# A tile's base product moved in among the expert tiles, and a split moved out of the layer that makes the data into the one that reads it

## The reference, cut to what matters

```python
def _L2_ffn_ref(x, base_w, base_b, A, B, router_w):
    base_out = jnp.einsum('bsi,oi->bso', x, base_w) + base_b
    res_hidden = jnp.einsum('bsi,ri->bsr', x, A)
    topw, topi = jax.lax.top_k(softmax(x @ router_w.T), 2)      # weights normalised, 16 experts
    delta = jnp.einsum('bse,bsr,eor->bso', combine, res_hidden, B)
    return base_out + delta * SCALING

def _L3_ffn_ref(hidden_states, ...):      # hidden_states = y3 = agg_w @ x + agg_b, channels mixed again
    h = jnp.maximum(hidden_states @ up_w, 0) ** 2
    shared_out = h @ down_w
    ...                                    # gates, latent experts
    return layernorm(shared_out + routed_out)

x = x + _L2_ffn_ref(...)
x = x + _L3_ffn_ref(_L3_cond_ref(x, ...), ...)
```

## Time and profile before

| | us |
|---|---|
| median of 3 runs | 1654.09 (1651.56 to 1657.61) |
| profiled execution | 1651.25 |
| its span, first to last instruction | 1649.5 |
| TensorE busy | 1576.2 (96%) |
| VectorE busy | 823.7 (50%) |
| ScalarE busy | 506.4 (31%) |
| GpSimd busy | 315.2 (19%) |
| mean granted clock of TensorE | 0.988 of 2.4 GHz |

### The profile page before, as it was taken

One profiled execution on the slowest core, in us unless ns is written; L12 is line 12 of the kernel. 1 busy time (PEld: TensorE's weight loads), 2 busy tenths in 40 slices (PEclk: granted clock), 3 DMA queues, 4 the chain that ended last, 5 costly groups with the idle time before them and its releaser, 6 DMA issues.

```text
span 1649.5 us, 20620 instructions
## 1 busy us (share of the span) xinstructions
PE 1576.2 (96%) x7752; PEld 1284.4 (78%) x7752; DVE 823.7 (50%) x1336; ACT 506.4 (31%) x761; POOL 315.2 (19%) x262
## 2 busy tenths in 40 slices
PE   7899879999998889999999999999999999999996
PEld 5688558889976558877888888887788888888875
DVE  4567578895374537772333333332723333333336
ACT  3344325333265521223222222212232222222122
POOL 1000022234155530122211111112112101111110
PEclk9999999999999999999999999999999999999999
DMA  9765635556774757894531111114925311111115
GB/s 308 224 197 166 139 97 182 167 186 212 243 241 126 288 194 291 301 321 155 111 92 51 51 51 51 51 52 140 319 77 100 83 49 51 51 51 51 52 41 177
DMA packets 117241, 238.57 MB, mean 145 GB/s; under 512 B 22503, under 2 KB 61551, under 8 KB 115778
## 3 DMA queue, kind: packets, MB, share of 16 engines
q1 hardware_dynamic: 80890, 154.75, 28.2%
q0 software_dynamic: 23008, 68.24, 13.8%
q10 hardware_dynamic: 13264, 14.52, 3.2%
HBM read 164.51 MB, written 89.19 MB: 154 GB/s over the span
## 4 chain that ended last, share of the span: by engine, by line
PE 77%; DVE 4%; POOL 2%; issue 2%; DMA 1%; ACT 1%; SPq 0%; ACTq 0%; DVEq 0%; POOLq 0%
PE pu L1956 27%; PE pd L1956 26%; PE l_po L1956 7%; PE pf L1956 6%; POOL scratch_pairs L1464 2%; PE l_ea L1313 2%; PE pw L648 2%; PE pw L647 2%; PE l_ea L1889 1%; PE l_po L1889 1%; PE pg L1085 1%; PE l_ea L1904 1%; PE l_tr L1904 1%; DMA scratch_g<-latent_out 1%; DMA scratch_expert_out<-expert_out,pair_ids 0%
## 5 line engine op out<-in xcount | busy, mean ns | idle before, releaser
L1956 PE MATMUL pd<-down_hi,hid_hi 128*128 128x512 f32 x640 | 249.1, 389 | 2.9 <-issue 2.9
L1956 PE MATMUL pu<-y_hi,up_hi 128*128 128x512 f32 x640 | 250.5, 391 | 0.6 <-issue 0.6
L1956 PE MATMUL pu<-y_lo,up_hi 128*128 128x512 f32 x640 | 250.3, 391 | 0.0
L1956 PE MATMUL pu<-y_hi,up_lo 128*128 128x512 f32 x640 | 250.3, 391 | 0.0
L1956 PE MATMUL pd<-down_hi,hid_lo 128*128 128x512 f32 x640 | 249.0, 389 | 0.0
L1956 PE MATMUL pd<-down_lo,hid_hi 128*128 128x512 f32 x640 | 249.0, 389 | 0.0
L2257 DVE TENSOR_TENSOR hid_lo<-hidden,hid_hi 128x512 fp32r<-128x512 f32 x64 | 44.3, 692 | 391.5 <-ACT hid_hi L2165 391.5
L2087 POOL TENSOR_TENSOR down_lo<-raw,down_hi 128x1024 fp32r<-128x1024 f32 x40 | 100.3, 2508 | 681.2 <-ACT down_hi L2102 681.2
L2159 ACT ACTIVATE hidden<-pu 128x512 f32<-128x512 f32 x64 | 38.3, 598 | 470.0 <-PE pu L1956 470.0
L2196 DVE TENSOR_TENSOR acc<-pd,acc 128x512 f32<-128x512 f32 x224 | 143.6, 686 | 54.7 <-PE pd L1956 51.4
L1956 PEld LDWEIGHTS pd<-down_hi,hid_hi 128*128 128x128 f32 x640 | 120.1, 188 | 28.8 <-issue 3.7
(11 more groups left out here) (324 smaller groups left out, 2494.5 us busy)
## 6 DMA issues: line engine op xcount, KB each, us to landing
l_x<-scratch_x SPq DMA_DIRECT2D x32, 512.0 KB, 6.5
delta<-scratch_expert_out SPq DMA_DIRECT2D x32, 512.0 KB, 6.8
raw<-in_up SPq DMA_DIRECT2D x32, 512.0 KB, 3.6
raw<-in_down SPq DMA_DIRECT2D x32, 512.0 KB, 4.3
X<-scratch_x SPq DMA_DIRECT2D x248, 64.0 KB, 2.6
y1T<-in_x SPq DMA_DIRECT2D x16, 512.0 KB, 9.8
scratch_x<-y1T SPq DMA_DIRECT2D x16, 512.0 KB, 3.0
scratch_x<-l_x SPq DMA_DIRECT2D x16, 512.0 KB, 5.5
```

Source lines behind the costliest of these rows:

```text
L1956: mm = pe.matmul(out, lhs[a], rhs[b], start=first and n == 0, stop=last and n == len(pairs) - 1)
```

## The change

1. Tile 7's base product is done in the experts' groups (`INSIDE = 7`). After each of groups 0 to 3 TensorE does one feature chunk of tile 6 (k from 4 to 7, two parts), after each of groups 4 to 11 one of tile 7 (k from 0 to 7), and the biases after groups 3 and 11. The loop then begins with tile 8: steps 0 to 7 have a base product, step 8 has only the mixes of 14 and 15. The loads and splits of y2 for tiles 7 and 8 move to groups 3, 4, 7, 8 and 9; base_out(6) moves into group 4; base_out(7) comes after the stage. SP asks for the x of tile 8 once the last group's rows are taken, then, after the tile before the last three, for those of 7 and 9.
2. y3 of tiles 8 to 15 isn't split any more where it is made. VectorE evicts it into one of four buffers, and POOL stores it once in `scratch_y3`.
3. In the middle of layer 3, POOL loads this y, unsplit, in two loads of 2 MB into `y_raw`, which lies where the low part goes. ScalarE casts it into `y[0]`, VectorE subtracts into `y[1]`, in pieces of 128x1024, four for each half of the columns. Those of the first half stand ahead of the first addition and the norms, those of the second half among tiles 1 and 2 on ScalarE and behind tiles 2 to 5 on VectorE.

```diff
-X3_AT = [2, 3, 5, 6, 0, 1, 13, 7, 8, 2, 3, 6, 5, 0, 8, 6]
+X3_AT = [2, 3, 5, 6, 0, 1, 13, None, 8, 7, 3, 6, 5, 0, 8, 6]
-X3_STEP = {1: (9, 10), 2: (11, 12), 3: (13,), 5: (14,), 6: (15,)}
+X3_STEP = {1: (10,), 2: (11, 12), 3: (13,), 5: (14,), 6: (15,)}
...
# sync, experts' stage and loop
         for g in range(3, NGRP):
             rows_in(g)
-            if g == 6:
-                y2_in(7, 1)
-        y2_in(8, 0)
-        sp.wait_ge(tr_mm, NGRP)
-        x3_in(7)
+            if g == 3:
+                y2_in(INSIDE, 1)
+            if g == 7:
+                y2_in(INSIDE + 1, 0)
+            if g == 9:
+                y2_in(INSIDE + 1, 1)
         sp.wait_ge(twice, NGRP)
         sp.wait_ge(row_ids, NGRP)
         x3_in(8)
+        sp.wait_ge(eo_mm, 8 * (NGRP - 1))
+        sp.wait_ge(r_lo, NGRP - 1)
+        x3_in(7)
+        sp.wait_ge(tr_mm, NGRP)
+        x3_in(9)
+        y2_in(INSIDE + 2, 0)
...
         for s in range(9):
-            if 9 + s < NT:
-                y2_in(9 + s, 0)
-            elif 9 + s == NT:
+            if 10 + s < NT:
+                y2_in(10 + s, 0)
+            elif 10 + s == NT:
                 sp.wait_ge(y2_lo, 2 * NT)
                 first["raw"](sp, 0)
...
# gpsimd: y3 of tile t, n = t - 8
-                    pool.wait_ge(y3_hi, t + 1)
-                    pool.dma_start(SC["y3"][0][:, :, n * P:(n + 1) * P],
-                                   y3h[y3_slot(t)][:].bitcast(F32).rearrange("p (k j) -> p k j", k=KC)).then_inc(y3_stored[t % 2], 16)
-                    pool.wait_ge(y3_lo, n + 1)
-                    pool.dma_start(SC["y3"][1][:, :, n * P:(n + 1) * P],
-                                   y3[y3_slot(t)][:].rearrange("p (k j) -> p k j", k=KC)).then_inc(y3_stored[t % 2], 16)
+                    pool.wait_ge(y3_made, 2 * (t + 1))
+                    pool.dma_start(SC["y3"][:, :, n * P:(n + 1) * P],
+                                   y3[n % 4][:].rearrange("p (k j) -> p k j", k=KC)).then_inc(y3_stored[n % 4], 16)
...
# vector
+                if n == 1 and g == 4:
+                    base_out(INSIDE - 1)
+            if g == 4:
+                y2_low(INSIDE, 1)
+            if g == 8:
+                y2_low(INSIDE + 1, 0)
+        y2_low(INSIDE + 1, 1)
+        base_out(INSIDE)
         for s in range(9):
             for t in mixed_tiles(s):
                 add_deltas(t)
...
-            base_out(7 + s)
+            if 8 + s < NT:
+                base_out(8 + s)
             for t in mixed_tiles(s):
                 y3_out(t)
             for t in mixed_tiles(s):
-                y3_low(t)
+                if t < NT // 2:
+                    y3_low(t)
...
# tensor
-            if g == 0:
-                base_start(6, 1)
-            if g < 8:
-                base_part(6, 4 + g // 2, g % 2)
-            if g == 8:
-                base_bias(6)
+            t, k = (INSIDE - 1, 4 + g) if g < 4 else (INSIDE, g - 4)
+            if k % 4 == 0:
+                base_start(t, k // 4)
+            for h in range(2):
+                last = base_part(t, k, h)
+            if k == 7:
+                base_bias(t)
+            elif k == 3:
+                last.then_inc(base_mm, 1)
         for s in range(9):
-            base_chunk(7 + s, 0)
-            base_chunk(7 + s, 1)
+            if 8 + s < NT:
+                base_chunk(8 + s, 0)
+                base_chunk(8 + s, 1)
             for t in mixed_tiles(s):
                 mix(t)
...
# layer 3, gpsimd
-                for part in range(2):
-                    pool.dma_start(y[part][:, :, cols], SC["y3"][part][:, :, cols]).then_inc(y_loaded[n], 16)
+                pool.dma_start(y_raw[:, :, cols], SC["y3"][:, :, cols]).then_inc(y_loaded[n], 16)
# layer 3, scalar
+        def y_high(n, c):
+            k, cols = y_piece(n, c)
+            act.wait_ge(y_loaded[n], 16)
+            act.copy(y[0][:, k, cols], y_raw[:, k, cols]).then_inc(y_hi, 1)
...
             for T in range(HT * half, HT * (half + 1)):
+                if again and T % HT in (1, 2):
+                    for c in range(2):
+                        y_high(1, 2 * (T % HT - 1) + c)
...
+                if front:
+                    for c in range(YP):
+                        y_high(0, c)
+                norm(half - 1, front)
# layer 3, vector
+        def y_low(n, c):
+            k, cols = y_piece(n, c)
+            dve.wait_ge(y_hi, YP * n + c + 1)
+            dve.tensor_tensor(y[1][:, k, cols], y_raw[:, k, cols], y[0][:, k, cols].bitcast(F32), ALU.subtract).then_inc(y_lo[n], 1)
...
             if end:
+                if front:
+                    for c in range(YP):
+                        y_low(0, c)
                 for t in range(HT):
...
+                    if front and 2 <= t < 2 + YP:
+                        y_low(1, t - 2)
```

More of the change, by code:

```diff
@@ L1255, in phase_l2 @@
     R1A, R1B, R2A = 15, 23, 36
-    mats_loaded, bias3_loaded, d_loaded, y3_stored, y_ready, y_loaded = [s_.slot_sems(n) for n in (
-        "mats3_loaded bias3_loaded delta_loaded y3_stored y_ready l2_y_loaded").split()]
+    INSIDE = 7
+    mats_loaded, bias3_loaded, d_loaded, y_ready, y_loaded = [s_.slot_sems(n) for n in (
+        "mats3_loaded bias3_loaded delta_loaded y_ready l2_y_loaded").split()]
+    y3_stored = s_.slot_sems("y3_stored", 4)
     x3_loaded, x3b_stored, eo_stored = s_.slot_sems("l2_x3_loaded", 4), s_.slot_sems("x3b_stored", 4), s_.slot_sems("expert_stored", 4)
@@ L1742, in y3_out @@
             dve.wait_ge(bias3_loaded[t % 2], 16 * (t // 2 + 1))
[L1743 to L1746 removed]
+            n = t - NT // 2
+            if n >= 4:
+                dve.wait_ge(y3_stored[n % 4], 16)
+            elif n >= 0:
+                old = {0: 5, 1: 6, 2: 9, 3: 7}[n]
+                dve.wait_ge(x3b_stored[old % 4], 16 * (old // 4 + 1))
             for h in range(2):
@@ L1806, in vector @@
                     row_numbers(g + 2)
-            if g == 9:
-                base_out(6)
-                y2_low(7, 1)
+                if n == 1 and g == 4:
+                    base_out(INSIDE - 1)
+            if g == 4:
+                y2_low(INSIDE, 1)
+            if g == 8:
+                y2_low(INSIDE + 1, 0)
+        y2_low(INSIDE + 1, 1)
+        base_out(INSIDE)
         for s in range(9):
@@ L1812, in vector @@
                 add_deltas(t)
+            if 9 + s < NT:
+                y2_low(9 + s, 0)
+                y2_low(9 + s, 1)
             if 8 + s < NT:
-                y2_low(8 + s, 0)
-                y2_low(8 + s, 1)
-            base_out(7 + s)
+                base_out(8 + s)
             for t in mixed_tiles(s):
@@ L1846, in base_bias @@
             for h in range(2):
-                last = pe.matmul(po[t % 2][h][:], K["ones_r"][0:BR, :], brow[:, chunk(h)], start=False, stop=True)
+                last = pe.matmul(po[bank(t)][h][:], K["ones_r"][0:BR, :], brow[:, chunk(h)], start=False, stop=True)
             last.then_inc(base_mm, 1)
@@ L2273, in y_there @@
             if half:
[L2274 removed]
+                pe.wait_ge(y_lo[n], YP)
             else:
@@ L2380, in build @@
     SC["mats"] = [nc.dram_tensor(f"scratch_mats{i}", (BATCH, CH * CH), F32).ap() for i in range(2)]
-    SC["y3"] = [nc.dram_tensor(f"scratch_y3_{part}", (P, KC, NT // 2 * P), F32).ap() for part in ("hi", "lo")]
+    SC["y3"] = nc.dram_tensor("scratch_y3", (P, KC, NT // 2 * P), F32).ap()
     SC["pairs"] = nc.dram_tensor("scratch_pairs", ((NEXP + 1) * P, RW), F32).ap()
```

95 lines of the change are left out of this document (39 added, 56 removed).

## The result

The changed kernel takes 1665.37 us (median of 5 runs, 1663.49 to 1668.4), the kernel before, run beside it, 1654.23: a ratio of 1.0077, 95% interval 1.0059 to 1.0094. It is slower by 11.1 us. The forecast was slower, 1661.2 us in a range of 1654 to 1667.

What follows compares the result with a forecast made beforehand. TensorE, busy 1576.2 of 1649.5 us, was taken as the bound. Experts +5.3, loop -8.7 and middle +10.5 made +7.1 on the profiled 1651.25, 1658.35; with that execution 2.84 under the median, the forecast was 1661.2, range 1654 to 1667.

Steps and rivals of the forecast that it cites:

- the end of part 2: Loop's end after base tile 15: 15.1 us to the first upward product, with 3.2 us of new TensorE waiting before mix 14.
- the clock in part 3: Middle of the last stage: granted clock 0.50 after TensorE's wait for the load, costing 1.7 us.
- Part 1: Experts' stage: 48 matmuls and one bias added, 11.5 us, less 5.8 of store wait; taken as +5.3 us.
- the store wait: End of the experts' stage: 5.8 us of waiting for an expert tile's store, expected to go.
- TensorE's idle time lies behind it and does not absorb it: Experts' groups: a base part ahead of the opening transposes costs its own length, despite 12.8 us of idle time.
- Rival B: Experts' stage absorbs all of tile 7's base work at no cost: sum +1.8, 1655.9 us; chance 0.12.
- Part 2: Base tiles and mixes: one base tile fewer, partly offset by new waits before the last mixes; -8.7 us.
- Rival C: End of the mixes: tile 14's deltas late, TensorE restarts at half clock; loop saves only 4, 1665.9 us; chance 0.16.
- Part 3: Middle of the last stage: TensorE waits 8.0 us behind y's load and split, plus clock and VectorE drift; +10.5 us.
- VectorE's drift: Middle, tiles 2 to 5: second-half subtractions exceed VectorE's idle time by 0.2 us each, 0.8 in all.
- Rival A: Middle: y's first load lands in 8.1 us, leaving 2.5 us of wait and no clock fall; 1654.0 us; chance 0.12.
- The row: Middle: profile row of an earlier y load landing in 13.6 us, used instead of the skill page's 6.8.

Runs made afterwards that it cites:

- base_in_gap: Changed kernel with each group's two base parts between its second and third tile, and base_out(6) at the end of group 3: 1658.27 us, ratio 1.0026.
- raw_later: Changed kernel with SP's load for the first upward weights behind the deltas of tiles 12 and 13: 1661.07 us, ratio 1.0043.
- early_load: Changed kernel with GpSimd issuing the first load of y ahead of its last subtraction of the down weights: 1653.16 us, ratio 1.0008.
- mid_pool: Changed kernel with GpSimd instead of VectorE doing the four subtractions of y's first half: 1663.98 us, ratio 1.0068.
- mid_act: mid_pool with ScalarE's first-half casts behind the first tile's norm and the second half's casts and subtractions two tiles later: 1658.43 us, ratio 1.0042.
- covered_tail: Changed kernel with the second half of base tile 15 behind mixes 12 and 13: 1671.92 us, ratio 1.0104.
- early_spread: Changed kernel with the edits of base_in_gap, raw_later, early_load and covered_tail, and VectorE's first-half subtractions spread: 1644.85 us, ratio 0.9948.

## Why the prediction was right, and where it was off

**Slower, and why.** The sum was +7.1, measured was +10.95 in the three stretches, less the opening's 1.85, for which the forecast had no term. The parts had the right signs and order, and the waits that it named were seen: with the first transposes' 4.3 us taken off, the first base tile starts at 607.6. Two terms were too small: the end of part 2 (by 3.0 us, of which the forecast had allowed for 0.6) and the clock in part 3 (by 1.4). The time of 1665.4 lies near the top of the range, beyond the forecast's own 1657 to 1665.

**Part 1** (+5.3): measured +5.66. Up to the last transposes the stage is 7.4 us longer (75.04 from 523.44 to 598.48, against 67.64), behind them 1.7 shorter (13.39 against 15.13) though 3.4 us of base work lies there. That the store wait and its half clock go is right: what is left of it is 0.82 us. "TensorE's idle time lies behind it and does not absorb it" is right for that place alone: between the second and third tile of a group nearly all of the same work is absorbed (68.5 us up to the last transposes against 67.6 before, base_in_gap). Rival B had the amount and not the place.

**Part 2** (-8.7): measured -6.13. The eight base tiles are as forecast, 115.56 against 115.4. Mis-sized was the end: 18.07 us to the first upward product instead of 15.1. Mix 14 began at 9.03 instead of 7.0, and took 3.55 instead of 1.98, which is the fall of the clock; mix 15 then had no wait left, -0.6. The prediction had counted the deltas (those of tile 14, asked for at 722.82, were there when their addition came) but not the matrices and the bias on ScalarE's queue. raw_later shows their price: with SP's load behind the deltas mix 14 begins at 7.45, near the 7.0 of the forecast, and the end is 16.6. The other 1.5 us are mostly the slow clock in mix 14 (3.65 us instead of 1.98), of which the forecast had only "a little". Rival C had the half clock and named the wrong load; its -4 was not reached.

**Part 3** (+10.5): measured +11.42. The wait was 8.15 against 8.0, the load 14.0 against 13.6. The third tile took 8.50 us instead of 5.44: the clock was 0.50 for 4.2 us and 0.78 for the next 4, so it cost 3.1 and not 1.7. VectorE's drift was 0.2 to 0.3 and not 0.8: the second half's subtractions, 1.13 us from start to start, nearly fit into its idle time. early_load shows the landing as the cause, by amount.

**Rival A**, the load lands in time, fell in the changed kernel. early_load has its outcome (a wait of 1.43 us), by an earlier issue and not by a fast landing. The Trainium skill (DMA: Bandwidth & Descriptors, section "Anatomy of one DMA - SWDGE (gpsimd) path") would have given 6.8 us for this load, an estimate from its figures; the runs have 14.0 and, issued 4.4 us earlier, 11.7. The row was the better guide. No run has the load alone, so that its neighbours on the other queues make the difference is not shown.

## What to carry to other kernels

An engine that is 96% busy can still be given work for almost nothing, if it is put exactly where that engine waits: 8.1 us of base parts cost 7.4 us behind the groups and 0.8 between their second and third tiles. To price it, compare a stretch in which the change did nothing else: over the whole stage, 82.0 against 82.8 us would have made it look free. When a long tile is taken away, go through all that it covered, small loads and the engine's own order included: each has its own lateness, and laying other work over one of them uncovers the next. And when a load gets a reader sooner, ask first if it can be issued sooner: one move on the issuing queue was worth 9.4 us in the middle here; moving the work behind the load to another engine gave 2.6, and 8.7 with ScalarE's order changed too.

## What the hardware did that I had not expected

**GpSimd beside VectorE.** While GpSimd subtracted two SBUF tensors, VectorE's scalar_tensor_tensor on SBUF tensors took 1.65 to 3.25 us instead of 1.28 (2.47 and 3.20 in mid_pool; 3.25, 1.65, 3.24 and 1.65 in mid_act), and the one with an input in PSUM, at 1161.55 in mid_act, its usual 0.74. GpSimd's four took 10.43 us in mid_pool and 13.44 in mid_act; one subtraction of that size takes it 2.48 elsewhere. The Trainium skill (SBUF - State Buffer, section "SBUF: two separate sides") says that the two engines share a port pair as a lock held for a whole instruction, which an operation of VectorE with two SBUF inputs needs too when the one of GpSimd reads SBUF. These rows agree as to which operations grow; they do not tell a lock from a shared rate.

**Small loads in a full stage.** The bias took 13.22 us to land in the changed kernel, with the DMA engines busy throughout (share 1.00, 375 GB/s from 719.3 to 732.5), and the matrices 11.88 in covered_tail. With SP's raw load put later, matrices landed in 3.92 us in raw_later and in 5.44 in early_spread, there with 336 GB/s beside them (712.7 to 718.1). So a small load is not a quick one in a full stage, and the rate alone doesn't tell how late it is.

**The clock after idle time.** After 3.7 us of idle the granted clock was 0.55 for the next 3.6 us, after 8.15 us it was 0.50 for 4.2 and 0.78 for another 4; after 1.43 us it did not fall. There is also a fall without a wait ahead of it: before the change, with 0.5 us of idle time in the loop, the clock was 0.83 for 10 us (760 to 770), some 20 us behind the loop, where 48 upward matmuls took 12.71 us; in the changed kernel, 1.00 and 11.10. That is most of the opening's 1.85 us. mid_pool, mid_act and early_load, which have the change, have the longer opening again (400.6). What decides it is open; no run tests it.
